# Units 0 and 1 make the next key earlier, unit 1 reads its placed blocks later, and the first loads are issued in another order

## The reference, cut to what matters

```python
x = x + _L0(x)   # x @ W.T + b + 2 * (x @ A[id]) @ B[id]          rank 16
x = x + _L1(x)   # x @ weight[id].T                                one 512x512 matrix per sequence
x = x + _L2(x)   # (x @ B[id].T) @ A[id].T                         rank 16
x = x + _L3(x)   # attention with a paged cache
```

```python
q, k, v = x @ Wq.T, x @ Wk.T, x @ Wv.T          # 32 query heads, 8 key heads, D = 128
q, k = rope(rmsnorm(q, q_norm_w)), rope(rmsnorm(k, k_norm_w))
k_all = concat([k_cache[block_table], k])        # 512 cached keys and 128 new ones
v_all = concat([v_cache[block_table], v])
scores = q @ k_all.T * SCALE                     # cached keys past the length are masked
out = (softmax(scores) @ v_all) @ Wo.T
```

## Time and profile before

| | |
|---|---|
| median of three runs | 1142.35 us |
| the profiled execution's own time | 1145.5 us |
| its span (first to last instruction) | 1143.8 us |
| PE busy | 1109.5 us, 97% of the span |
| DVE, ACT, POOL busy | 867.5, 697.3, 478.8 us |
| mean granted TensorE clock | 0.991 of 2.4 GHz |

### The profile page before, as it was taken

How to read it: one execution, slowest core, us unless ns; L and a number is a source line. 1 busy time by engine, 2 the same in 40 slices (tenths; PEclk the granted TensorE clock), 3 DMA queues, 4 the chain that set the end, 5 groups by cost and what they waited for, 6 DMA issues and landing times.

```text
span 1143.8 us, 27449 instructions
## 1 busy us (share of the span) xinstructions
PE 1109.5 (97%) x6116; PEld 972.0 (85%) x6116; DVE 867.5 (76%) x2203; ACT 697.3 (61%) x1949; POOL 478.8 (42%) x570
## 2 busy tenths in 40 slices
PE   5999699999999999999999999999999999999998
PEld 3656588888888889898898988989888888889886
DVE  3568778877787877778777887778877788777773
ACT  2344556766666666666666676666766666666663
POOL 6855334444344444344443444444444444432330
PEclk9999899999999999999999999999999999999999
DMA  6694577887778878787887887877888878777883
GB/s 180 211 310 164 176 233 252 260 256 242 256 246 270 254 235 259 246 273 248 243 255 247 266 251 249 252 255 252 259 252 246 255 254 264 234 222 227 245 249 99
DMA packets 125331, 275.77 MB, mean 241 GB/s; under 512 B 14076, under 2 KB 78716, under 8 KB 124290
## 3 DMA queue, kind: packets, MB, share of 16 engines
q1 hardware_dynamic: 78736, 193.37, 48.7%
q10 hardware_dynamic: 35426, 45.49, 16.1%
q0 software_dynamic: 11152, 36.72, 12.3%
HBM read 186.67 MB, written 88.87 MB: 241 GB/s over the span
## 4 chain that ended last, share of the span: by engine, by line
PE 85%; DMA 4%; DVE 1%; ACT 1%; issue 1%; POOL 0%; ACTq 0%; SPq 0%; DVEq 0%; POOLq 0%
PE ps_o L1008 23%; PE ps_q L943 15%; PE ps_kv L943 8%; PE ps_s L853 6%; PE ps_s L851 6%; PE ps_s L852 6%; PE ps_o L852 5%; PE ps_o L851 5%; PE ps_o L853 5%; DMA prob_t<-blocks_placed 2%; PE ps_q L972 2%; PE ps_x L964 2%; DMA blocks_placed<-blocks 2%; PE ps_kv L973 1%; DVE blocks L1339 1%
## 5 line engine op out<-in xcount | busy, mean ns | idle before, releaser
L767 ACT ACTIVATE prob<-prob,low 128x640 f32<-128x640 f32 x256 | 210.3, 827 | 156.8 <-DVE low L1315 148.3
L1315 DVE CUSTOM_DVE_ANT_0 prob<-ps_s,mask,q_gain 128x640 f32<-128x640 f32 x256 | 215.5, 879 | 34.3 <-PE ps_s L853 34.1
L1008 PE MATMUL ps_o<-prob_t,v_raw 128*128 128x256 f32 x992 | 236.0, 381 | 0.6 <-DMA prob_t<-blocks_placed 0.4
L1339 DVE STREAM_TRANSPOSE blocks<-prob 128x640 f32<-128x640 f32 x252 | 204.1, 829 | 1.8 <-ACT prob L772 1.8
L1008 PEld LDWEIGHTS ps_o<-prob_t,v_raw 128*128 128x128 f32 x992 | 184.5, 191 | 23.8 <-issue 1.0
L772 ACT ACTIVATE prob<-prob,inv 128x640 f32<-128x640 f32 x256 | 196.5, 815 | 0.0
L851 PE MATMUL ps_s<-kt_hi,qt_hi 128*128 (+1 forms) x512 | 171.1, 334 | 3.8 <-DVE kt_lo L1236 2.3
L943 PE MATMUL ps_q<-w_hi,x_s 128*128 (+1 forms) x512 | 171.5, 395 | 0.0
L853 PE MATMUL ps_s<-kt_hi,qt_lo 128*128 (+1 forms) x512 | 159.5, 311 | 0.0
L852 PE MATMUL ps_s<-kt_lo,qt_hi 128*128 (+1 forms) x512 | 159.0, 311 | 0.0
L720 ACT ACTIVATE ot_hi<-ps_o 128x256 fp32r<-128x256 f32 x128 | 49.0, 383 | 162.3 <-PE ps_o L1008 155.5
(11 more groups left out here) (194 smaller groups left out, 2256.2 us busy)
## 6 DMA issues: line engine op xcount, KB each, us to landing
blocks_placed<-blocks SPq DMA_DIRECT2D x126, 640.0 KB, 3.9
prob_t<-blocks_placed ACTq DMA_DIRECT2D x126, 320.0 KB, 5.6
prob_t<-blocks_placed SPq DMA_DIRECT2D x126, 320.0 KB, 6.4
x_s<-xt_split SPq DMA_DIRECT2D x64, 512.0 KB, 3.7
w_raw<-w_qkvo_dram SPq DMA_DIRECT2D x55, 320.0 KB, 3.8
w<-w_t_dram SPq DMA_DIRECT2D x8, 1024.0 KB, 6.8
xt_split<-x3t ACTq DMA_DIRECT2D x8, 512.0 KB, 5.3
w_raw<-w_qkvo_dram POOLq DMA_DIRECT2D x9, 320.0 KB, 6.3
```

What stands on the lines that cost most here:

```text
L767: nc.scalar.activation(prob[:, h, :], prob[:, h, :], ACT.Exp, bias=low[:, h:h + 1], scale=-1.0, accum_out=total[:, h:h + 1]).then_inc(exp_ ...
L1008: mm = nc.tensor.matmul(ps_o[pair][:, 0:PAIR], v, turned_probs(c, pair), start=c == 0, stop=c == CH - 1)
L1315: nc.vector.tensor_tensor_reduce(out=prob[:, h, :], in0=ps_s[:, score_slot(h):score_slot(h) + KEYS], in1=mask[:, :], scale=q_gain[:, h:h + ...
L1339: nc.vector.transpose(blocks[:, h // 2, :, :, h % 2, :].rearrange("p j c q -> p c j q"), prob[:, h, :].rearrange("p (c j k) -> p c j k", c ...
```

## The change

There are three edits.

1. SP no longer loads `xbt[:, 1]` behind `w0`; that load stands behind `w1`. The two lists of ids are issued by ACT at its start instead of by SP.
2. POOL waits for the last quarter of `w0` before it issues its six table loads.
3. In units 0 and 1 (`early=True`) DVE makes the variances and rotates the next key before it turns any block, and turns the blocks of heads 2 and 3 after the low parts. ACT scales the next key before the second pair of exponentials, makes the high parts before the second pair of normalizations, and in unit 1 issues `place_rest(0)` behind `scale_key(2)` instead of at its start.

```diff
@@ SP, the opening
                     for k in range(KT):
                         sp.dma_start(w0_raw[:, k, :], w0_t[:, k, :]).then_inc(w0_in[k], 16)
-                    sp.dma_start(xbt[:, 1, :], one(x_t, 1)).then_inc(xt_in[1], 16)
                     sp.wait_ge(stacks_set, 1)
...
                     first_input(0, 0, first=True)
-                    sp.dma_start(ids[:, 1, :], ids1).then_inc(other_ids_in, 16)
-                    sp.dma_start(ids[:, 2, :], ids2).then_inc(other_ids_in, 16)
                     sp.dma_start(ident[:, :], ident_in).then_inc(ident_in_place, 16)
                     sp.wait_ge(other_ids_in, 32)
                     second_weights(0, 0, first=True)
+                    sp.dma_start(xbt[:, 1, :], one(x_t, 1)).then_inc(xt_in[1], 16)
                     first_input(0, 1, first=True)
@@ POOL, the opening
                     nc.gpsimd.memset(neg_half[:, :], -0.5)
+                    pool.wait_ge(w0_in[KT - 1], 16)
                     pool.dma_start(len_i[:, :], lens.partition_broadcast(P)).then_inc(tables_in, 16)
@@ ACT
                     act.dma_start(ids[:, 0, :], ids0).then_inc(ids_in, 16)
+                    act.dma_start(ids[:, 1, :], ids1).then_inc(other_ids_in, 16)
+                    act.dma_start(ids[:, 2, :], ids2).then_inc(other_ids_in, 16)
...
-                        if out:
+                        if out and not early:
                             place_rest(n - 1, first=not head)
                         exps(n, 0)
                         exps(n, 1)
...
                             new_value(n + 1, first=not out)
+                        if early:
+                            scale_key(n + 1)
+                        if out and early:
+                            place_rest(n - 1, first=not head)
                         if third:
                             third_turned(B - 1)
                             store(B - 1)
                         exps(n, 2)
                         exps(n, 3)
-                        if not last:
+                        if early:
+                            cached_high(n + 1, first=not out)
+                            rotated_high(n + 1)
+                        elif not last:
                             scale_key(n + 1)
                         normalize(n, 2)
                         normalize(n, 3)
-                        if not last:
+                        if not last and not early:
                             cached_high(n + 1, first=not out)
                             rotated_high(n + 1)
...
-                    step(0, False, head=False, out=False, third=True)
-                    step(1, False, head=False)
+                    step(0, False, head=False, out=False, third=True, early=True)
+                    step(1, False, head=False, early=True)
@@ DVE
                         lowest(n, 3)
+                        if early:
+                            variances(n + 1)
+                            rotate_key(n + 1)
                         if first:
                             third_turned(B - 1)
                         if not last:
                             turn_blocks(n, 0, first)
+                        if not last and not early:
                             variances(n + 1)
                             rotate_key(n + 1)
+                        if not last:
                             turn_blocks(n, 1)
                         inverse(n, 2)
                         inverse(n, 3)
+                        if early:
+                            cached_low(n + 1)
+                            rotated_low(n + 1)
+                            gains(n + 1)
...
                             turn_blocks(n, 2)
                             turn_blocks(n, 3)
+                        if not last and not early:
                             cached_low(n + 1)
```

More of the change, by code:

```diff
@@ L783, in keep_turned, with step @@
                         copy(last_home(pair, i), last_banks[pair][i]).then_inc(last_kept_act, 1)
-                    def step(n, last, head=True, out=True, first=False, third=False):
+                    def step(n, last, head=True, out=True, first=False, third=False, early=False):
                         if head:
                             out_high(n - 2, 1, first=first)
-                        if out:
+                        if out and not early:
                             place_rest(n - 1, first=not head)
@@ L1340, in turn_blocks, with step @@
                                             prob[:, h, :].rearrange("p (c j k) -> p c j k", c=CH, j=NB)).then_inc(blocks_turned, 1)
-                    def step(n, weights, last, head=True, out=True, first=False):
+                    def step(n, weights, last, head=True, out=True, first=False, early=False):
                         if head:
@@ L1420, in _ @@
                     set_mask(0)
-                    step(0, True, False, head=False, out=False, first=True)
-                    step(1, True, False, head=False)
+                    step(0, True, False, head=False, out=False, first=True, early=True)
+                    step(1, True, False, head=False, early=True)
                     with dve.Fori(2, UNITS - AHEAD) as n:
```

## The result

The changed kernel took 1156.68 us (median of 6 runs, 1155.84 to 1162.29), the kernel before 1142.38 us on the same chip (6 runs, 1141.11 to 1143.85). The medians differ by 14.3 us, where 2.4 were predicted. The ratio, here of the mean times, is 1.0133 with a 95% interval of 1.0112 to 1.0153, which would be 15.2 us: the mean takes in the slowest run. 1156.68 lies outside the range, beyond the rival in which POOL's chain sets the start of phase 2.

What follows compares the result with a forecast made beforehand. PE bounds the kernel from 160 us on, so early microseconds count fully. Opening -1.0, unit 0 +0.1 and unit 1 +3.3 sum to +2.4 us: 1144.8 us on the median, 8-in-10 range 1141.0 to 1147.9.

Steps and rivals of the forecast that it cites:

- the rival in which POOL's chain sets the start of phase 2: Tables land after 9.8 us beside `w1`, POOL's eighth chunk 3.8 us behind PE's present start: about 1148.3 us, 10 in 100.
- the landing of POOL's tables: Opening: the last table, issued at 10.2, lands in 5.0 us, at 15.2, 0.8 us later than before.
- the clock behind the new wait for POOL: First projection of phase 2: PE waits 0.7 us for POOL; no slower clock behind that wait was priced.
- the landing of `prob_t`: Unit 1: ACT's transfers land 4.5 us after issue, so `values(0)` starts at 147.1, 3.3 us lost.
- the later store of the last sequence: Unit 0: store 2.0 us later, unit 2's input counted as just in time; otherwise the upper bound, 0.8 us lost.
- The opening: Before phase 2: PE gains 1.7 us but waits 0.7 for POOL, so 1.0 us won; ends 1.9 won, 5.5 lost.
- the cover of POOL: First projection of phase 2: POOL's eighth chunk was ready 1.75 us before PE started; the change was to use it up.
- the calm row: Profile row of a 320 KB POOL load landing in 4.3 us on a calmer queue, guiding the 5.0 us for the tables.
- The second turned input: Opening: `xbt[:, 1]` travels behind `w1`; PE's second sequence starts at 19.3 or 23.0 instead of 21.39, 1.7 us won taken.
- Unit 0: PE's wait only changes place, shorter before the turn and longer behind: 0.1 us lost, bounds 0.5 won and 0.8 lost.
- Unit 1: PE turns 0.8 us earlier, then waits for `prob_t` at `values(0)`: 3.3 us lost, ends 1.7 and 5.7 lost.
- The 0.8 us that the turn of unit 2 was to win: Unit 1: one transposition fewer ahead on DVE brings the key's scaling, and PE's turn, 0.8 us earlier.

Runs made afterwards that it cites:

- a3: The kernel before with SP's new order of loads alone (second turned input behind `w1`, ids on ACT): 1140.14 us, ratio 0.9997.
- b1: The kernel before with SP's new order of loads, and POOL beginning the angles after two of its six tables: 1139.73 us, ratio 0.9979 to the kernel before.
- b2: b1 with ACT, in unit 1, issuing `place_rest(0)` behind the first two exponentials and normalizations: 1138.68 us, ratio 0.9983 to the kernel before.
- a4_keys_only: The kernel before with the new key order in units 0 and 1 alone, `place_rest(0)` and all loads as before: 1146.2 us, ratio 1.0042.
- a2: The kernel before with POOL's wait for the last quarter of `w0` alone: 1144.23 us, ratio 1.0031.
- u2: The changed kernel with `place_rest(0)` back at the start of unit 1, POOL's wait kept: 1153.45 us, ratio 1.0091 to the kernel before.
- u3: The changed kernel without POOL's wait and with `place_rest(0)` back at the start of unit 1: 1143.89 us, ratio 1.0017 to the kernel before.
- s1: a4_keys_only with the last sequence's copy, store and low part back in front of the key work: 1142.36 us, ratio 1.0019 to the kernel before.
- t1: The changed kernel with SP holding `w1` and all loads behind it until POOL's six tables are in: 1151.3 us, ratio 1.0085 to the kernel before.
- w1_pe_kept_busy: The changed kernel with 36 identity turns on PE ahead of its wait for phase 2's first weights: 1156.6 us, ratio 1.0130 to the kernel before.
- s2: The kernel before with the new key order in unit 0 alone, unit 1 as before: 1144.97 us, ratio 1.0037.

## Why the prediction was wrong

Four terms failed, all by their size or by being put at nothing: the landing of POOL's tables (5.0 us taken, 9.9 measured), the clock behind the new wait for POOL (nothing, 2.65 us), the landing of `prob_t` (4.5, 6.9), and the later store of the last sequence (0.8 us at most, 3.7 in the stretch where it stands alone).

**The opening (-1.0; measured +5.7, and 2.65 behind it).** Right were the quick landing of `w0`, the short bias issues (234 to 313 ns) and the cover of POOL: PE did wait for it. The reason given for the short issues, four large loads ahead of SP instead of five, was not: with the same four the long issue is back in a3, b1 and b2. Wrong was the landing of the tables. I took 5.0 us "near the calm row" and held that what made them slow was mostly `w0`. It was whatever large load was beside them: the change that took `w0` away brought `w1` from 17.16 forward to 9.75, on top of the tables. I had `w1` issued at 10.8 and the last table at 10.2, and named `w1` among the new neighbours, but priced the landing as if it were not there. With 9.9 us instead of 5.0 the working gives POOL at 20.1 (measured 20.45) and a loss of about 4.0. This was the rival to which I gave 10 in 100. Its 3.8 us were short by 1.9: POOL began 6.1 us later instead of 5.6, and its chain took 1.3 us more on the way to the eighth chunk, which was ready at 104.41 instead of 97.04.

The second turned input was also mis-sized: 8.5 us of PE's wait, a start at 22.74 where I had 19.7 (the bound was 23.0). It travels behind `w1` beside the tables. It cost nothing more only since POOL was later still: PE stood at the first projection at 97.9.

**The clock (0; measured 2.65).** I did not apply what I said of `values(0)` to the first projection, which had no wait before. Its twelve matmuls took 5.49 us from the first start to the last end, at 0.80 and 0.63 each, instead of 3.05 us. From projection to scores 0 it is 15.24 to 16.19 us in the four kernels in which PE waits 2.7 to 7.7 us for POOL, 13.39 to 13.46 in those with no wait there or one of 1.20 us, and 13.41 with PE kept busy. (In a4_keys_only, 14.74, PE had waited 2.54 us just ahead of the projections.) The Trainium skill (TensorE: Matmul & The Clock Gate, The HAM clock gate) says that the throttled state is the default and that activity releases it; these rows agree, and by it the price of a new wait ahead of warm work should have stood in the sum.

Of `values(0)` I said that the slower clock behind a wait is in the trace already and costs nothing new. Against the one trace that I had read this came out (17.32 and 17.49 us to `values(1)`), but by luck: that execution stood at 0.57 there without a wait, and a2, a3 and b1, with the same units, take 15.8. Against them the term is 1.5 us.

**Unit 0 (+0.1; measured 0.0).** Scores 0 to scores 1 take 17.26 instead of 17.30. The wait changed its place, as worked out: 2.32 before the turn, 4.59 behind it.

**Unit 1 (+3.3; measured +6.4).** The wait for `prob_t`, its place and its cause were right; u2 and u3 show it by its absence. These sizes were off:

- The store. I wrote that it would come 2.0 us later, and the input of unit 2 and the blocks with it, and priced only the input. Issued 2.0 us later (13.03 against 11.00 after scores 0), it held the blocks back by 3.4 us (25.98 against 22.55), since it also took 4.4 us to land instead of 2.65. Where ACT still waits for the blocks this is the largest part of what the key order costs: 3.7 us of the stretch between a4 and s1. In the changed kernel itself ACT comes to them 4.6 us after they are back, and the store acts through the input of unit 2, in the next point.
- The 0.8 us that the turn of unit 2 was to win did not come (13.84 against 13.70 after scores 1): the input of unit 2 was 1.05 us late, and ACT had the scaling only at 151.07. So ACT's issue of `prob_t` stood at 13.3 after scores 1 instead of 12.7.
- The landing took 6.9 us, which is the upper end of the earlier trace rows, instead of my 4.5 (the four landed in 3.7, 5.2 in the median and 6.9). That I took the lower end since "only two are under way" was a guess: SP's two were issued 4.6 us earlier and were just landing, with two loads of unit 3 behind them. Which of these made ACT's slow no run tells.

0.6 for the later issue and 2.4 for the landing make the 3.3 a 6.3.

The chain of waits of the changed kernel from 140 to 160 us shows what the issue stood behind:

```profile
142.27 3.07 PE ps_q L951 x12
...
146.80 1.30 POOL rot L543
...
149.79 1.21 POOL rstd L547
...
151.07 0.37 ACT rot L742
...
151.47 6.89 DMA prob_t<-blocks_placed
```

**How the parts add.** One at a time: loads 0, POOL's wait 3.5, keys 4.8. The late placing was never tried without the keys; with the 4.8 to 5.5 us that it has beside them the parts make 13 to 14 of the 15.2. From the changed kernel downward it is 7.8 for POOL's wait, 5.5 for the late placing, 1.9 for loads and keys. With some 2 us of doubt on each, only POOL's wait is clearly dearer in one order than in the other, and the traces say why: the new order of the loads puts `w1` beside the tables.

What stays open: why the late store also lands late. From its issue to SP's `step(0)` it is 4.1 to 4.4 us in all eight kernels that have it late, and 2.65 in the six others. POOL issues a gather of cached rows 0.8 to 1.1 us ahead of it in the eight and 2.3 to 3.0 us behind it in the six, but no run moved the gather alone. Open too is why the late placing costs 4.8 to 5.5 us by the ratios and 2.3 to 3.2 in the stretches.

## What to carry to other kernels

When an edit removes a transfer from beside another, ask what moves up into the gap, and price the landing by the slowest row with a neighbour of that size. When an edit reorders an engine's work, follow each DMA issue in it to what the queue behind it holds: here a store that nobody on the engine waits for came back two units later, through SP and a round trip through DRAM. A wait for a semaphore that counts six loads is a wait for the slowest of them; split by who needs what first, it let POOL begin at 10.03 us instead of 12.83 here, though a gain in time isn't shown. And a state that one trace shows, a slow clock or a long issue, may be of that execution alone: read a second one before it becomes a term.

## What the runs showed of the hardware

- A 64 KB load issued by POOL as the last of six landed in 4.8 us with no large load beside it (t1), in 5.0 with 1024 KB issued 2.4 us behind it (a2), in 7.9, 8.5 and 9.9 us beside 1024 KB and 256 KB of SP (w1_pe_kept_busy, u2, the changed kernel), and in 6.2 to 9.9 us beside the four quarters of `w0` in the nine kernels that have it there. In the other direction the quarters landed in a median of 4.2 to 4.6 us without the tables and of 5.3 to 9.9 beside them.
- Twelve projections behind a wait of 6.6 us ran at a granted clock of 0.50 and took 5.49 us, and 3.05 without a wait. A wait of 2.71 us did the same (s2), and one of 1.20 did not (a3).
- One SP issue among six bias rows took 3.1 to 4.1 us in before, a3, b1, b2 and s2, and none was over 0.8 us in the other nine kernels. In the five where POOL's loads wait for `w0` it was never there; in the nine others it comes and goes, so one trace doesn't tell whether an edit removed it.
